# Two further matmuls of 392 columns before each batch of the sort's placing step

## The reference

```python
q = (X @ Wq)[src]
k = (X @ Wk)[dst]
e = jnp.tanh(q + k)
scores = e @ Wphi
scores = scores - jnp.max(scores)
exp_scores = jnp.exp(scores)
denom = jax.ops.segment_sum(exp_scores, src, num_segments=N)
alpha = exp_scores / (denom[src] + 1e-09)
vy = (X @ Wy_w + Wy_b)[dst]
ve = e @ We
msg = alpha[:, None] * (vy + ve)
out = jax.ops.segment_sum(msg, src, num_segments=N)
# result: _layernorm(x + out)
```

## Time and profile before

| | |
|---|---|
| median of the runs | 5648.86 us |
| the profiled execution's own time | 5649.77 us |
| its span, first to last instruction | 5648.0 us |
| mean granted clock of TensorE | 0.748 of 2.4 GHz |
| TensorE busy (share of the span) | 4178.2 us (74%) |
| VectorE busy | 3638.0 us (64%) |
| GpSimd busy | 3497.5 us (62%) |
| ScalarE busy | 2776.5 us (49%) |

### The profile page before, as it was taken

One profiled execution on the slowest core, in us unless ns is written; L12 is line 12 of the kernel. 1 busy time (PEld: TensorE's weight loads), 2 busy tenths in 40 slices (PEclk: granted clock), 3 DMA queues, 4 the chain that ended last, 5 costly groups with the idle time before them and its releaser, 6 DMA issues. The chain is left out here.

```text
span 5648.0 us, 99340 instructions
## 1 busy us (share of the span) xinstructions
PE 4178.2 (74%) x26293; PEld 3164.3 (56%) x26293; DVE 3638.0 (64%) x8199; ACT 2776.5 (49%) x10974; POOL 3497.5 (62%) x3560
## 2 busy tenths in 40 slices
PE   7899999995676666666666666666766666676677
PEld 6745555553555555555555555555555555555556
DVE  6588888886555555555555555555555555655556
ACT  3488888884343344444444444444444434434346
POOL 1022333233777777777777777777777777777771
PEclk9956666665877777777777777778777777777778
DMA  2200000002333333333333333333333333333334
GB/s 85 70 4 4 4 4 5 4 4 59 105 105 105 105 104 105 105 105 105 105 105 105 105 105 105 105 105 105 105 106 105 105 104 105 105 105 105 105 98 108
DMA packets 279601, 478.59 MB, mean 85 GB/s; under 512 B 91964, under 2 KB 198878, under 8 KB 278814
## 3 DMA queue, kind: packets, MB, share of 16 engines
q0 software_dynamic: 166144, 326.27, 21.7%
q1 hardware_dynamic: 95132, 140.96, 7.8%
q10 hardware_dynamic: 17794, 4.91, 0.4%
HBM read 456.42 MB, written 20.60 MB: 84 GB/s over the span
## 5 line engine op out<-in xcount | busy, mean ns | idle before, releaser
L1015 POOL DMA_INDIRECT gathered<-table,dst_rows x3296 | 3156.7, 958 | 1035.0 <-issue 967.3
L1050 PE MATMUL bank<-gathered,weighted_onehots 128*128 128x193 f32 x6592 | 1793.8, 432 | 364.1 <-DVE block_sums L1122 350.4
L1039 PE MATMUL bank<-q_parts,src_onehots_T 128*128 x9888 | 1136.3, 216 | 983.9 <-DVE src_onehots_T L1084 728.8
L1050 PEld LDWEIGHTS bank<-gathered,weighted_onehots 128*128 128x128 f32 x6592 | 1497.5, 255 | 420.9 <-ACT weighted_onehots L1070 347.1
L1039 PEld LDWEIGHTS bank<-q_parts,src_onehots_T 128*128 128x128 bf16 x9888 | 870.0, 107 | 1410.0 <-issue 1208.6
L1122 DVE TENSOR_TENSOR block_sums<-block_sums,bank 128x193 f32 x3296 | 1166.1, 354 | 527.3 <-issue 193.6
L1059 ACT ACTIVATE gathered<-gathered 128x256 f32<-128x256 f32 x824 | 346.0, 420 | 2190.3 <-DVE gathered L1098 2190.3
L1070 ACT ACTIVATE weighted_onehots<-src_onehots,edge_weight 128x128 f32<-128x128 bf16 x3296 | 1073.4, 396 | 26.8
L1098 DVE TENSOR_TENSOR gathered<-bank,gathered 128x256 f32<-128x256 f32 x824 | 349.5, 424 | 1125.8 <-DMA gathered<-table,dst_rows 1107.6
L797 ACT ACTIVATE places_past_far<-bank,stat 128x98 bf16<-128x98 f32 x2727 | 887.3, 401 | 130.0 <-DVE place_col L780 93.0
L839 POOL DMA_INDIRECT sorted_list<-sorted_groups,unit_destinations x248 | 319.7, 1289 | 813.3 <-DVE sorted_groups L767 749.5
(11 more groups left out here) (180 smaller groups left out, 2248.7 us busy)
## 6 DMA issues: line engine op xcount, KB each, us to landing
src_in_block_rows<-src_in_block_list SPq DMA_DIRECT2D x206, 512.0 KB, 3.8
gathered<-table,dst_rows POOLq DMA_INDIRECT x3296
table<-in_x SPq DMA_DIRECT2D x4, 1562.5 KB
x_in<-in_x SPq DMA_DIRECT2D x24, 256.0 KB, 2.9
x_again<-in_x SPq DMA_DIRECT2D x48, 128.0 KB, 2.3
out<-out_rows SPq DMA_DIRECT2D x48, 128.0 KB, 1.9
sorted_list<-sorted_groups,unit_destinations POOLq DMA_INDIRECT x248, 2.5
table<-k_and_q ACTq DMA_DIRECT2D x24, 128.0 KB, 2.0
```

The source lines that it names most:

```text
L1015: e.indirect_dma_start(slot[:, r, j, 0:ROW], None, table, bass.IndirectOffsetOnAxis(ap=gidx[:, t:t + 1].bitcast(u32), axis=0)).then_inc(ga ...
L1039: made = e.matmul(QK[q % 2][:, j * A:(j + 1) * A], ohT[:, c % 2, o:o + PARTS], q3[:, bass.ds(b + s_ * A, A)], start=s_ == 0, stop=s_ == 2)
L1050: made = e.matmul(SM[q % 2 * 2 + j // 2][:, o:o + SUMS], ohw[:, q % 3, j, :], slot[:, r, j, A:SLOT], start=True, stop=True)
```

## The change

Ahead of each batch, behind the wait for its bank, TensorE multiplies `before` with the batch's one-hots twice, each with `start=True, stop=True`, into the same 392 columns. L821 then begins the same bank anew (`start=True`), so nothing of the two products is read. No semaphore, wait or other engine is touched.

```diff
--- before.py
+++ after.py
@@ -818,6 +818,8 @@
                             was = reader_of[b - len(PL)]
                             e.wait_ge(places_read_vector if was in by_vector else places_read_scalar, by_vector[was] + 1 if was in by_vector else by_scalar[was] + 1)
                         h0 = t0 - c * SORT_CHUNK
+                        for _ in range(2):
+                            e.matmul(o, before[:, :], hot[:, g % 2, c, h0 // PB, :, 0:mt].rearrange("p b t -> p t b"), start=True, stop=True)
                         e.matmul(o, ones[0:2, :], flat[:, g % FLATS, t0:t0 + mt, :], start=True, stop=False)
                         e.matmul(o, before_far[:, :], hot[:, g % 2, c, h0 // PB, :, 0:mt].rearrange("p b t -> p t b"), start=False, stop=True).then_inc(placed, 1)
                 elif what == "add":
```

## The result

The changed kernel takes 6200.98 us at the median, the kernel before 5648.43 beside it: a ratio of 1.098, 95% interval 1.0967 to 1.0998, or 552.6 us more. The forecast was 6370 with a range from 6230 to 6430, so the sign and the place were right and the price of the two matmuls was too high: 552.6 us where 720 were forecast. One of the four executions of the kernel before took 12187.95 us and stands outside the comparison.

The account below looks back on a forecast made before the run. The prediction took TensorE's own steps, which fill the whole sort, to bound the kernel. It summed 5650 us now, 704 for the new matmuls and 16 for the clock to 6370 us, range 6230 to 6430.

Parts of the forecast that it names:

- The forecast's own sign of being wrong: The prediction is wrong if the sort's stretch grows by under 580 us or over 780, or the main stage behind changes length.
- Item 2: In the sort on TensorE, each of 1612 new matmuls costs L822's step of 0.437 us, 704 us in all.
- The lower bound of item 2: New matmuls in the sort at L829's cost per column, with loads hidden: 0.36 us each, 583 us in all.
- The rule of the Trainium skill: Next weights load while the current matmul streams; N / 1.2 ns at the low clock: 0.327 us each, 527 us, so 6193.
- the clock term of +16: Extra us in the sort, between equal high-clock time and equally many L821 at the high clock.
- the loads hide between equal weights: Rival: in the sort both new matmuls, sharing one stationary matrix, hide their loads at 0.36 us each: 6249 us; chance 0.12.
- Item 4: In the sort, fewer L821 fall into the high clock, partly offset by denser row use: +16 us.
- The other side: Rival: the high clock makes the sort's matmuls cheap enough to pay for the new two, 0.163 us each, 5523 us; chance 0.03.

Follow-up runs that it names:

- x1: The changed kernel with one new matmul per batch instead of two: 6640.15 us, ratio 1.0443 to the kernel before.
- x6: The changed kernel with its two new matmuls multiplying two rows of base places by ones instead of the one-hots: 6870.64 us, ratio 1.0798 to the kernel before.
- x7: The kernel before with its batches in twos, both first matmuls and then both second ones, nothing added: 5557.93 us, ratio 0.9846.
- x10: x3 with the two new matmuls reading their columns packed, not with a step of four: 5677.86 us, ratio 1.0068 to the kernel before.
- x3: The changed kernel with the base places in a tile of 128 rows, rows 2 to 127 zero: 6694.20 us, ratio 1.0528 to the kernel before.

## Why the prediction was wrong in size

- **What bounds the kernel, and where the time lies: right.** The whole cost is in the sort's stretch (555 us of 553), TensorE has no idle time in it, ScalarE's grew, and the stages before and behind it are as long as they were to 2 us. The forecast's own sign of being wrong, a stretch that grows by under 580 us, came. Each load of weights was issued, too: 1612 more matmuls and 1612 more loads.
- **Item 2, the price of one new matmul, failed.** It was 0.437 us for each, 704 us, and measured 0.35 each, 0.70 a pair, 560 us. I took L822's step as the price of a matmul like it. But that step belongs to the order: it holds the load of the two-row matrix that stands behind it. Each batch has two exposed loads before and after the change, whatever stands between them, and x1, x6 and x7 show that it is the changes that count. The text had the right observation, that L829's loads hide and those of L821 and L822 don't, and asked no further what differs between them. The answer stood in its own rows: from the L822 at 707.32 to the L829 at 707.65 there are 0.33 us at the low clock, as both matrices have 128 rows, and the text took off 0.44 there "for the L822 itself".
- **The lower bound of item 2 was no bound.** 0.118 us for a matmul of 128 columns was scaled to 392 columns as 0.36. Of the 0.118, a part doesn't grow with the columns: 392 columns take 0.327 at the low clock. With 583 us as its lower end and the low end of the range worked out from it, the range could not hold the result. Rows that give some 0.33 were there: the L822 at 707.32, and 0.437 less one load of 0.107.
- **The rule of the Trainium skill was set aside too fast.** From "TensorE: Matmul & The Clock Gate", section "Back-to-back issue gap", the text worked out 527 us and 6193 in all, 8 us from the result, and called it contradicted by the pair. That the time came so near is in part luck: 527 is 33 us short of the 560 that the new matmuls took, and the clock term of +16, which measured -3, made up for more than half of it. The rule that loads run beside the current matmul (section "Step-by-step: what each phase is for") agrees with the trace for steps between two matrices of 128 rows or two of 2, and disagrees where 2 and 128 alternate: 0.33 and 0.44 in the same batch.
- **The rival "the loads hide between equal weights" was near, with 0.12, and for another reason.** It gave 6249 with hidden loads for both. x1 and the step from L824 to the next batch show that equal weights are not the condition.
- **Item 4, the clock: small, and the sign was off.** Forecast +16 us; the mean L823 gives some -3. The share of L823 at the high clock did not fall, as batches stay at the high clock for more microseconds than before (granted 0.65 against 0.62).
- **The other side.** Its price of 0.17 us for 392 columns at the high clock exists, but needs two things that the change doesn't bring: 128 rows in every matmul, so that the loads hide and the clock stays high, and packed columns. x10 has both but for L829, and its batch of four takes 0.85 us (600.51 to 601.36), 0.04 above the average pair of before.

What stays open: what exactly holds the clock down in this sort. The granted clock in 300 to 900 us was 0.55 with three of four matmuls on two rows, 0.62 with one of two, 0.66 with one of three (x1), 0.65 with one of four, 0.65 with 64 rows, 0.94 with 100 and 0.97 to 1.00 with 128 rows. Open too are the 0.02 us by which a new matmul exceeds its columns, and the exact border between 64 and 100 rows. The rows in use and the exposed loads change together in most of these runs. Halving the exposed loads alone (x7) left it at 0.63, which speaks for the rows; going from 2 to 64 rows with the loads still exposed gained only 0.03, which speaks for the loads. No run separates the two.

## What to carry to other kernels

The step between two matmuls is a property of the pair. Before pricing an added one by a row, see which matrices stand on both sides of it: where a small stationary matrix alternates with a full one, each change exposed a load of 0.11 us here, and giving it 100 or 128 rows in place of 2, the added rows of its moving operand zero, took 131 us off a kernel of 5640 (100 rows) and 129 off one of 6365 (128 rows). A bound that is scaled from a small matmul to a large one is no bound unless its fixed part is taken off.

## What was not expected of the hardware

- The load of a stationary matrix hid behind the running matmul (step 0.327 us for 392 columns at the low clock) with 128 and 128, 100 and 128, and 2 and 2 rows, and was exposed (0.44) with 2 and 128 and with 64 and 128. In f32, 65 and 128 rows alternated at no extra cost (0.21 us a matmul of 128 columns).
- A moving operand with a step of four bf16 elements took 0.33 us for 392 columns at either clock; packed, the same columns took 0.17 at the high clock. x3 and x10 differ in this alone, besides the chip.
- With 128 rows in place of 2 in the first matmul of a batch, the added moving rows zero, the granted clock in 300 to 900 us rose from 0.62 to 0.97.
